# A gated delta-product layer and its experts on one core: blocks ordered by time and head, a new pipeline order, and a shorter inverse

## What is computed

```
q, k, v = silu(causal conv of 4 taps(x @ W))      # k and v three times per token
beta = 2 sigmoid(x @ Wb);  g = -exp(A_log) softplus(x @ Wa + dt_bias)
q = l2norm(q) / sqrt(128);  k = l2norm(k)
for every token:   S = S * exp(g)
    for i in 0..2: S = S + beta_i k_i (v_i - k_i S)
    o = q S
out = (o * rsqrt(mean(o^2) + 1e-5) * rms_weight * silu(x @ Wg)) @ Wo
```

## Time and profile before

| | |
|---|---|
| median of 3 runs | 5084.51 us (5080.6 to 5097.39) |
| profiled execution | 5080.19 us, its span 5078.4 us |
| busy: PE / PEld | 4474.4 us (88%) / 3959.6 us (78%) |
| busy: DVE / ACT / POOL | 3659.4 us (72%) / 3570.6 us (70%) / 1354.3 us (27%) |
| instructions | 150544 |
| DMA | 474.05 MB, mean 93 GB/s |

### The profile page before, as it was taken

How to read it: one execution, slowest core, us unless ns; L and a number is a source line. 1 busy time by engine, 2 the same in 40 slices (tenths; PEclk the granted TensorE clock), 3 DMA queues, 4 the chain that set the end, 5 groups by cost and what they waited for, 6 DMA issues and landing times. The chain is left out here.

```text
span 5078.4 us, 150544 instructions
## 1 busy us (share of the span) xinstructions
PE 4474.4 (88%) x50436; PEld 3959.6 (78%) x50436; DVE 3659.4 (72%) x9814; ACT 3570.6 (70%) x8898; POOL 1354.3 (27%) x1231
## 2 busy tenths in 40 slices
PE   1799999999999999999999999999999966599991
PEld 0688888888888888888888888888888845488881
DVE  3788888878888878888888888788888722344445
ACT  2688888878888878888878888778888711255551
POOL 2223333333333333333333333322222202200004
PEclk6999999999999999999999999999999988699996
DMA  4322222222222322222222222222222123366663
GB/s 196 85 59 71 71 74 80 78 70 74 72 72 72 81 69 82 72 72 72 80 70 82 72 72 71 74 63 65 57 57 57 35 84 106 120 234 234 234 232 114
DMA packets 322317, 474.05 MB, mean 93 GB/s; under 512 B 85888, under 2 KB 267136, under 8 KB 302720
## 3 DMA queue, kind: packets, MB, share of 16 engines
q1 hardware_dynamic: 304784, 437.06, 29.4%
q0 software_dynamic: 6144, 16.79, 1.0%
q10 hardware_dynamic: 10608, 10.23, 0.6%
HBM read 352.02 MB, written 107.75 MB: 91 GB/s over the span
## 5 line engine op out<-in xcount | busy, mean ns | idle before, releaser
L1087 DVE SCALAR_TENSOR_TENSOR conv_acc<-bank,c_cur,conv_acc 128x256 f32<-128x256 f32 x2688 | 1283.0, 477 | 23.4 <-ACT conv_acc L899 4.2
L611 PE MATMUL bank<-x_cur,w_cur 128*128 128x259 f16 (+1 forms) x6144 | 855.4, 275 | 69.5 <-DMA g_cur<-g_parts 66.0
L957 ACT ACTIVATE inv<-bank 128x256 f16<-128x256 f32 x1536 | 606.8, 395 | 262.2 <-PE bank L704 241.0
L1258 POOL TENSOR_TENSOR squares<-kq_t 128x1024 f32<-128x1024 f32 x128 | 242.3, 1893 | 1704.6 <-ACT kq_t L911 1704.6
L1144 DVE CAST_PREDICATED xs_lev<-mask,bank 128x256 f16<-128x256 uint16 x1536 | 657.9, 428 | 53.4 <-PE bank L693 5.7
L611 PEld LDWEIGHTS bank<-x_cur,w_cur 128*128 128x128 f16 (+1 forms) x6144 | 588.4, 102 | 137.3 <-DMA g_cur<-g_parts 66.9
L755 PE MATMUL bank<-state,kq_t 128*128 128x128 f32 x2048 | 472.7, 313 | 136.2 <-DVE state L1157 107.6
L1251 POOL TENSOR_TENSOR decay<-decay_tok,cst 128x512 f32<-128x512 f32 x256 | 319.3, 1268 | 948.3 <-ACT decay_tok L923 948.3
L965 ACT ACTIVATE invt<-bank 128x256 f16<-128x256 f32 x1280 | 509.0, 398 | 24.2 <-PE bank L719 0.8
L899 ACT ACTIVATE conv_acc<-bank,c_cur 128x256 f32<-128x256 f32 x896 | 420.7, 469 | 143.2 <-PE bank L611 143.2
L1157 DVE SCALAR_TENSOR_TENSOR state<-state,t_cur,bank 128x128 f32<-128x128 f32 x1024 | 351.3, 343 | 217.5 <-PE bank L777 213.5
(11 more groups left out here) (249 smaller groups left out, 11045.7 us busy)
## 6 DMA issues: line engine op xcount, KB each, us to landing
w_cur<-w_parts_scratch SPq DMA_DIRECT2D x128, 1024.0 KB, 6.8
ew<-e_parts_scratch SPq DMA_DIRECT2D x117, 896.0 KB, 6.2
x_cur<-x_parts_scratch SPq DMA_DIRECT2D x128, 259.0 KB, 7.0
x_slots<-no_rows SPq DMA_DIRECT2D x128, 256.0 KB, 6.3
e_parts_scratch<-e_pair SPq DMA_DIRECT2D x96, 224.0 KB, 3.9
y_scratch<-y_buf SPq DMA_DIRECT2D x128, 128.0 KB, 3.3
y_in<-y_scratch SPq DMA_DIRECT2D x32, 512.0 KB
rows<-x_slots SPq DMA_DIRECT2D x39, 256.0 KB, 5.4
```

The source lines that it names most:

```text
L611: last = mm(bank[c % 2][:, 0:PW], w_cur[res][:, wp, k, c * P:(c + 1) * P].bitcast(BF16 if wp else F16), x_cur[res][:, xp, k, 0:PW].bitcast ...
L957: a(half(inv[g][:], l, 0), packed(halves(bank[4 + g]), l), ACT.Copy).then_inc(t_kept, 1)
L1087: v.scalar_tensor_tensor(acc, bank[c % 2][:, i:i + TB], c_cur[res][:, c, i:i + 1], acc, ALU.mult, ALU.add).then_inc(tap_step if i < TAPS - ...
```

## The change

The blocks go time, head-and-sequence: all 16 chains advance by 256 tokens, then the next 256. Sixteen states are kept in SBUF. A block's chain is spread over three bodies (units 0 to 2 in stage 1, 3 to 7 in stage 2, the last update in stage 3), so two chains are in flight. The Gram matrix and the first levels of group 0 move into stage 0. Every engine has a new order. The semaphore values come from a table of each order (`Count`). PSUM banks are given by kind: 2 for Gram, norms and turns, 3 for `level_x` and `fix`, 4 for `level_t`, 5 for `level_tt`, residual, decays and variance, 6 and 7 each for one chain and its outputs. The shared PSUM banks have one buffer.

```diff
-RING = 3
-PEELED = 8
-UNROLL = 24
+UNROLL = 32
...
-            state = sb("state", [P, P], F32)
+            state = sb("state", [P, B * H, P], F32)
...
-    masks = np.stack([masks[0].T] + masks[1:], 1).astype(np.float16)
+    masks = np.stack([masks[0].T.astype(np.float32) - np.eye(P)] + masks[1:], 1).astype(np.float16)
```

```diff
-                            mm(flat, ident16[:], rep16[:].rearrange("p a b -> p (a b)"), start=True, stop=False)
-                            mm(flat, negid16[:], inv[g][:].rearrange("p a b -> p (a b)"), start=False, stop=False)
+                            mm(dst, n_high[k.i % 2][g][:, u], by, start=True, stop=False)
+                            last = mm(dst, n_low[g][:, u], by, start=False, stop=True)
...
-                            mm(flat, ident16[:], invt[g][:].rearrange("p a b -> p (a b)"), start=True, stop=False)
+                            last = mm(LEVX[:, u * P:(u + 1) * P], xs[g][:, u], invt[k.i % R_LEV][g][:, u], start=True, stop=True)
...
-                            v.copy_predicated(half(first[g][:], 0, 1),
+                        v.tensor_tensor(half(first[g][:], 0, 1), half(n_high[k.i % 2][g][:], 0, 1),
+                                        half(mask4[:, 0], 0, 1), ALU.mult).then_inc(first_made.sem, 1)
...
+                        v.scalar_tensor_tensor(inv_t[k.i % R_INV][:, 4 * g:4 * g + 4].rearrange("p a b -> p (a b)"),
+                                               invt[k.i % R_LEV][g][:].rearrange("p a b -> p (a b)"), 2.0, LEVX[:],
+                                               ALU.mult, ALU.add).then_inc(x_kept.sem, 1)
...
+                    def minus_one(g, k):
+                        done(pool, rows_kept, ("gram", g), k.n)
+                        tt(n_t[g][:], n_t[g][:], cst[:, C_ID, None, :].broadcast_to([P, 4, P]), ALU.subtract)\
```

The variance. ScalarE copies the outputs to SBUF (`keep_out`, where it squared them), POOL squares them (`out_square`), squares the queries (`square_q`, cut out of `square`) and sums the two (`out_sum`), and one product takes the place of two:

```diff
-                            mm(VAR, over_dh[:], o_sq[:], start=True, stop=False)
-                            mm(VAR, eps_dh[:], squares[rc][:, :, 3, :], start=False, stop=True).then_inc(var_made, 1)
+                        mm(LEVTT[:, 0:TB], eps_dh[:], o_sum[:], start=True, stop=True).then_inc(tt_made.sem, 1)
```

`solve` now issues the short output product and then the solve; `update` of unit 7 also waits for `keep_out`. TensorE's new body (k0 is block n, k1 block n-1, and so on), cut:

```diff
+                        update(2, k2)
+                        turn_keys(0, k1)
+                        update(7, k3)
+                        level_x(1, 1, k1)
+                        project(1, k0)
+                        from_state(3, k2)
+                        level_tt(3, 0, k1)
+                        level_x(4, 0, k1)
...
+                        gram(0, k0)
+                        level_tt(4, 1, k1)
+                        level_x(5, 1, k1)
+                        solve(0, k1)
+                        project(5, k0)
+                        update(5, k2)
+                        update(0, k1)
+                        gram(1, k0)
+                        from_state(6, k2)
+                        from_state(1, k1)
+                        level_t(5, 1, k1)
+                        project(6, k0)
+                        level_tt(5, 1, k1)
+                        solve(6, k2)
+                        turn_first(0, k0)
+                        level_x(6, 1, k1)
+                        solve(1, k1)
+                        update(6, k2)
+                        level_t(6, 1, k1)
+                        level_x(1, 0, k0)
+                        level_tt(6, 1, k1)
+                        update(1, k1)
...
+                        turn_first(1, k0)
+                        variance(k2)
+                        fix(1, k1)
+                        level_t(3, 0, k0)
```

ScalarE's new body, from its start and at its end; the request for the joint table is gone:

```diff
-                        nc.scalar.preload_act_table_set("natural_log_exp_and_others")
...
+                        high(0, k1)
+                        keep_t(5, 1, k2)
+                        first_tap(5, k1)
+                        keep_tt(5, 1, k2)
+                        keep_w(6, k3)
+                        keep_first(0, k1)
+                        key_root(k1)
+                        keep_w(1, k2)
+                        keep_t(6, 1, k2)
+                        keep_tt(6, 1, k2)
+                        first_tap(6, k1)
+                        keep_t(1, 0, k1)
+                        keep_tt(1, 0, k1)
+                        keep_out(k3)
+                        high(1, k1)
+                        keep_res(1, k2)
+                        keep_w(7, k3)
+                        keep_t(2, 0, k1)
+                        keep_tt(2, 0, k1)
+                        keep_w(2, k2)
+                        keep_first(1, k1)
+                        var_ln(k3)
+                        silu(5, k1)
+                        keep_t(3, 0, k1)
...
+                        silu(0, k0)
+                        var_root(k3)
+                        exp_decay(k0)
+                        keep_w(5, k2)
+                        silu(4, k0)
+                        keep_w(0, k1)
+                        keep_tt(4, 1, k1)
+                        key_ln(k0)
```

1475 lines of the change are left out of this document (747 added, 728 removed).

## The result

The changed kernel takes **5183.45 us** (median of 4 runs, 5178.54 to 5200.73) against 5082.56 us before (median of 4, 5077.55 to 5097.39): a ratio of 1.020, 95% interval 1.0167 to 1.0232. It is slower by 101 us where I forecast 150 us less; the time lies just inside the upper end of the range that I gave (4700 to 5190), on the other side of the kernel before. The profiled run of it is the longest of the four, 5200.73 us, with a span of 5198.5, 120.1 us above the span before.

What follows compares the result with a forecast made beforehand. TensorE was taken to bound the loop. Per block, 25.6 us of its slots + 2.7 for two table places + 1.0 of remaining waits = 29.3 us against 30.49, over 128 blocks -152 us: 4930 us, range 4700 to 5190.

Steps and rivals of the forecast that it cites:

- Six loads of 1.28 us: On ScalarE: six table changes per block where there were two, each load holding the engine 1.28 us.
- the two places at `update` and `level_x`: Loads at key_root and var_ln delay ScalarE copies that TensorE's update(1) and level_x(4,0) need: 2.7 us per block.
- the state wait: TensorE's idle time ahead of the state product, about 0.8 us per block, goes with two chains in flight.
- GpSimd below half: GpSimd's added subtractions and squares bring it to 14 us per block, less than half the period.
- `fix` at 0.7: On VectorE: each of two new 512-wide fixes from PSUM taken at 0.7 us, bounds 0.6 and 0.9.
- the queues and the store of n-4: SP's earlier loads, other waits and the block order cost nothing; some 19 us are spare.
- TensorE's work 27.0 us: TensorE's busy time per block falls from 28.8 by 1.8 to 27.0 us as identity and variance products go.
- The step that failed: TensorE's other waits: a third of today's 3.1 us stays, 1.0 us per block; chain waits go, the rest partly overlaps.
- the base: TensorE's order priced by slots: 25.6 us per block new, 27.35 old, with 3.1 us of the old period being waits.
- Rival B: ScalarE becomes the bound, waits at level copies lengthening the period: 31.4 us per block, 5197 us, chance 0.20.
- Rival C: Even: today's waits all stay and loads eat TensorE's saving: 30.4 us per block, 5070 us, chance 0.10.
- Rivals A and D: A: the two placed loads absent or free, 4660 us, chance 0.13; D: loads cost about twice, 5480 us, chance 0.02.

Runs made afterwards that it cites:

- 5 loads: Changed kernel with the joint Ln and Exp table requested ahead of key_root, leaving five table loads per block: 4985.67 us, ratio 0.9812.
- 4 loads: Changed kernel with the joint Ln and Exp table requested ahead of key_ln, leaving four table loads per block: 4851.7 us, ratio 0.9546.
- two loads: Changed kernel with silu(4) ahead of exp_decay, joint table requested there, var_root moved ahead of next key_ln, normalize moved to VectorE's end: 5191.89 us, ratio 1.0211.
- (none): Kernel with four table loads per block, every Ln and Exp of the loop replaced by a copy: 4766.69 us, ratio 0.9384.
- the moved pair: Kernel with four table loads per block plus a joint-table request between silu(1) and silu(2), making six: 5104.03 us, ratio 1.0024.

## Why the prediction was wrong, and where it was right

**Right, with its size.** Six loads of 1.28 us on the lines that were named; the two places at `update` and `level_x`, 2.7 us per block said, 2.65 by their waits (1.47 and 1.18) and 2.39 measured by undoing them; the state wait gone; GpSimd below half; `fix` at 0.7 (0.68); the queues and the store of n-4 without a trace in the waits; TensorE's work 27.0 us by busy time said and 27.2 measured. A load holds ScalarE for what its row says: the instruction ahead ends at 646.52, the load starts at 646.54, and the next one starts at 647.83, 1.29 us later. The two places gave back 1.26 and 1.13 us when one load went at each. So nothing is seen to drain beside it, and the 2.66 us of the Trainium skill ("ScalarE: Activation LUTs", What ACT_TABLE_LOAD costs) is not what these traces show. The rule of the Trainium skill ("ScalarE: Activation LUTs", Table sets: the hidden batching unit) that ln, then exp takes one load was not so where no set was named (128 loads each at lines 963 and 969), and was so once the joint set was named.

**The step that failed** is the last term of the sum: "1.0 (a third of today's 3.1 us of waits; chain waits go, the rest overlaps partly with the new ones)". The waits beside the two table places came to 1.95 us per block. The traces show it when TensorE's time is split by slots: for each idle stretch, what the last product ahead of it counts as busy beyond its own slot (0.16 us, as at 647.09 above) belongs to the wait and not to the work.

| early stretch, us per step | step | idle | tails ahead of it | waits | work by slots |
|---|---|---|---|---|---|
| before | 30.33 | 1.55 | 1.23 | 2.8 | 27.55 |
| changed, 6 loads | 30.48 | 3.29 | 1.31 | 4.6 | 25.88 |
| 5 loads | 29.22 | 1.98 | 1.12 | 3.1 | 26.13 |
| 4 loads | 28.09 | 0.88 | 0.96 | 1.8 | 26.25 |

So the base was right: 27.35 us priced and 27.55 measured before, 25.6 priced and 25.9 measured after, and today's 3.1 us were nearly all waits. The early step of the changed kernel is 25.9 + 2.65 + 1.95 = 30.5. I let two thirds of today's waits go without naming what would stand in each place of the new order. The largest one did go: the update's way to the next state product, 0.99 us with its tail. But in the new order TensorE stops at six places that I had priced at nothing or did not list: for `rhs` at the solve 0.57 us (the normalization ahead of it on VectorE), at the norms behind the decays 0.31, at the solve of another unit 0.30, at a `level_tt` 0.26, at `fix` behind the variance 0.21, at a second `level_x` 0.20. All but the first are short idle times, 0.15 us and less, each with its 0.16 us of tail. In the four-load kernel 1.8 us of such waits are still there. Why each of the short ones stands where it does was not tried. The table's last column grows by 0.37 us from six loads to four: a product that waits for less than the tail ahead of it shows no idle time, and such waits, if there are any, count as work here.

**What was not in the sum at all.** (1) Stops and dips: the mean step is 31.17 where the early one is 30.48; the lower clock makes 0.44 of it by its record and the stops ahead of it most of the rest. Before, it is 30.49 against 30.33. I left the granted clock at 1.00; the row says 0.98. (2) The normalization: I let `keep_out` change the place of its input from PSUM to SBUF and cost that at nothing; standing behind GpSimd it cost 0.57 us per block, mostly the wait for `rhs` above. (3) The first block, 27 us later, with one more stage to fill; I had said 10 us for both ends, it was 34.5. (4) `first_level` at 0.415 instead of 0.3; VectorE had the room.

In sum, for the profiled run: 5200.7 - 4928 = 273 us, of which steps (31.17 - 29.3) x 127 = 237 and the ends 35. Per block the steps' 1.87 are +0.3 (work by slots, 25.9 for 25.6), +0.95 (other waits, 1.95 for 1.0), -0.05 (the two places) and +0.7 (dips and stops). The luck in it: at `level_x` my own terms, 4.3 us against 3.1, give 1.2, and I summed 1.4 to 1.5; undoing it gave 1.26.

**Rival B** gave 5197 us, close to what came, by a sum whose first part holds: ScalarE is the busiest engine in the loop (28.1 of 31.2 us), and 28.5 us of work with 2.0 of waits is the early step of the changed kernel. But its mechanism, every 0.1 us of wait at a level copy being 0.1 us of period because ScalarE is full, did not show: TensorE stands at the two places that the loads push, more work on TensorE alone lengthens the period of the same six-load kernel, and where ScalarE's work fell to 23.1 us (two loads) or 20.6 (none) the period did not follow. Its 31.4 us per block is near the mean of 31.17 by other terms; the 0.7 us of dips and stops are not in it. **Rival C** was the nearest account, at a chance of 0.10: its sum, 25.6 + 2.7 + 2.1 = 30.4, has every term within 0.3 of the early step's 25.9, 2.65 and 1.95. Its words are not its sum, though: they let all of today's 3.1 us stay, and with 3.1 it would be 31.4 us and 5197. Rivals A and D fell with the loads' rows and with the two kernels that took one and two of them out.

**What stays open.** What makes TensorE stand for "issue" in the middle of a body: a shorter body makes it more frequent, a longer one rarer, but without any loop 10 dips remain, and no run told apart the supply of instructions from other causes. Nor is it known why the changed order has more of these stops than the one before, or than the one with the moved pair, which differs from it by the place of two loads.

## What to carry to other kernels

Price an order by slots, and take everything by which today's period exceeds them as waits: the profile's busy time hid 1.2 of 2.8 us of them here, in the tails of the products ahead. Then do not let a share of them go in bulk; find the place of each in the new order, above all where a short product is followed by one that needs another engine. When an engine's table, or an operand's place, changes without a line that says so, follow what stands behind that instruction on its queue: here one line that names the joint table is worth 330 us, and one moved normalization 73 in the changed kernel and 35 with four loads. Look at the granted clock by stretches: the stop of 3.94 us shown above was followed by 13.7 us at the lower level, half of which, some 7 us (an estimate from the two levels), is more than the stop.

## What the hardware showed that I had not expected

- A VectorE instruction with its inputs in SBUF stood until a GpSimd instruction had ended: 1.42 us (median) in place of 0.47, over 1 us in 106 of 128 blocks, and 0.47 at a place where GpSimd was idle. The Trainium skill ("SBUF — State Buffer", Who interferes with whom) says that the port pair which the two share is an exclusive lock, and that a VectorE instruction with two SBUF inputs contends with a GpSimd instruction that reads SBUF; the traces agree. The same operation with its input in PSUM took 0.48 us before.
- The granted clock fell to its lower level during a stop of TensorE (3.94 us, above) and stayed there while the engine was again busy without a gap. Between the first normalization and the 125th the kernel before shows 24 us of it, in 5 dips near its loop's turns; the changed one 113 us in 19.
- The same instructions in bodies of 16, 32 and 64 blocks took 4950, 4852 and 4811 us.
